# Moving the evacuation of the attention accumulators, in the first half of the keys, from VectorE to ScalarE

## What is computed

```python
def polymax(x):            # on the causal scores, 1/DIVISOR = 1e-3
    x <= 0 and x >= -100:  (-0.01 * x + 1) / 1000
    x > 0:                 (x * x + 1) / 1000

x = x + attention(layernorm(x)) @ W_proj        # 16 heads of 64, causal, polymax in place of softmax
x = x + (gelu(layernorm(x) @ U1 @ V1 + b1) @ U2 @ V2 + b2)
```

## Time and profile before

| | us |
|---|---|
| median of two runs | 2102.88 (2097.38 to 2108.37) |
| the profiled execution, its own time | 2102.51 |
| its span on the slowest core, core 3 | 2101.0 (others from 2082.8) |
| busy on that core: TensorE, VectorE, ScalarE | 1305.7, 1260.8, 760.1 |

### The profile page before, as it was taken

One profiled execution on the slowest core, in us unless ns is written; L12 is line 12 of the kernel. 1 busy time (PEld: TensorE's weight loads), 2 busy tenths in 40 slices (PEclk: granted clock), 3 DMA queues, 4 the chain that ended last, 5 costly groups with the idle time before them and its releaser, 6 DMA issues.

```text
span 2101.0 us, 22691 instructions; the slowest of 8 cores (2082.8 to 2101.0 us)
## 1 busy us (share of the span) xinstructions
PE 1305.7 (62%) x6880; PEld 459.8 (22%) x6880; DVE 1260.8 (60%) x2171; ACT 760.1 (36%) x1074; POOL 0.2 (0%) x4
## 2 busy tenths in 40 slices
PE   2423295577786776777678337666765461468886
PEld 0001042243222222212112113322221220023332
DVE  3557432234888898889889523488997233344422
ACT  1100000000656676667667300176775000033332
POOL 0000000000000000000000000000000000000000
PEclk8655597889756677778777669855666685579998
DMA  5545202200000000000000320000000443001111
GB/s 165 160 120 180 100 7 73 74 7 11 21 8 19 16 6 16 8 16 6 16 18 6 96 69 1 1 1 1 1 1 23 158 147 113 0 0 41 40 41 40
DMA packets 53334, 96.07 MB, mean 46 GB/s; under 512 B 2529, under 2 KB 24290, under 8 KB 53218
## 3 DMA queue, kind: packets, MB, share of 16 engines
q1 hardware_dynamic: 46498, 84.14, 12.6%
q10 hardware_dynamic: 6720, 10.49, 1.7%
HBM read 82.04 MB, written 12.58 MB: 45 GB/s over the span
## 4 chain that ended last, share of the span: by engine, by line
PE 46%; DVE 25%; issue 13%; DMA 11%; ACT 3%; SPq 1%; DVEq 1%; ACTq 0%
DVE poolD L765 12%; PE ps L799 8%; DMA poolD<-W_attn 6%; PE ps L731 5%; PE ps L848 4%; PE ps L1124 3%; PE ps L933 3%; PE ps L1030 3%; PE ps L632 3%; PE ps L654 3%; PE ps L612 3%; PE ps L1144 3%; DMA poolD<-W_proj 1%; DMA poolD<-x_t 1%; DVE poolC L498 1%
## 5 line engine op out<-in xcount | busy, mean ns | idle before, releaser
L752 ACT ACTIVATE poolD<-ps 128x1024 bf16<-128x1024 f32 (+3 forms) x640 | 559.9, 900 | 849.0 <-PE ps L731 737.0
L765 DVE SCALAR_TENSOR_TENSOR poolD<-poolD 128x1024 bf16<-128x1024 bf16 (+3 forms) x640 | 653.0, 1058 | 43.4 <-ACT poolD L752 20.9
L799 PE MATMUL ps<-poolD,poolA 128*64 128x512 bf16 (+3 forms) x1280 | 298.4, 454 | 223.1 <-DVE poolD L765 115.4
L731 PE MATMUL ps<-poolB,poolA 64*128 64x512 bf16 (+3 forms) x1280 | 274.1, 454 | 35.7 <-ACT poolD L757 17.9
L799 PEld LDWEIGHTS ps<-poolD,poolA 128*64 128x64 bf16 x1280 | 89.0, 117 | 403.2 <-issue 401.7
L1136 ACT ACTIVATE poolC<-ps,sb_b1s 128x512 bf16<-128x512 f32 x128 | 87.7, 687 | 113.2 <-PE ps L1124 71.6
L757 ACT ACTIVATE poolD<-ps,consts 128x256 bf16<-128x256 f32 x256 | 123.7, 483 | 0.0
L848 PE MATMUL ps<-poolC,poolD 128*128 128x512 bf16 x256 | 123.1, 481 | 0.0
L731 PEld LDWEIGHTS ps<-poolB,poolA 64*128 64x128 bf16 x1280 | 64.2, 101 | 234.3 <-issue 233.5
L933 PE MATMUL ps<-poolD,poolC 128*128 128x512 bf16 x256 | 63.4, 405 | 55.4 <-DVE poolD L905 55.4
L612 PE MATMUL ps<-poolC,poolD 128*128 128x512 bf16 x256 | 57.1, 387 | 42.0 <-DVE poolD L591 42.0
(11 more groups left out here) (101 smaller groups left out, 1142.2 us busy)
## 6 DMA issues: line engine op xcount, KB each, us to landing
poolD<-x_t SPq DMA_DIRECT2D x8, 2048.0 KB, 10.3
poolA<-x_t SPq DMA_DIRECT2D x8, 2048.0 KB, 10.6
poolD<-W_attn SPq DMA_DIRECT2D x12, 1024.0 KB, 5.0
poolD<-W_attn SPq DMA_DIRECT2D x16, 512.0 KB, 4.1
poolC<-x_own_t SPq DMA_DIRECT2D x8, 1024.0 KB, 5.1
y<-poolC SPq DMA_DIRECT2D x4, 2048.0 KB, 6.8
kf2scratch<-poolD SPq DMA_DIRECT2D x32, 128.0 KB, 1.7
poolA<-kf2scratch SPq DMA_DIRECT2D x4, 1024.0 KB, 13.8
```

Of the source, the lines that this page charges most:

```text
L731: e.matmul(o, l, r, skip_group_check=True, start=True, stop=True, tile_position=tp),
L752: e.activation(o, i, AF.Relu), inc="S")
L765: e.scalar_tensor_tensor(o, i, 0.01, i, ALU.add, ALU.mult),
L799: e.matmul(o, l, r, skip_group_check=True, start=st, stop=True, tile_position=tp),
```

## The change

In half 0 the four pieces of the accumulator are evacuated by ScalarE in place of VectorE: as an activation `Identity` with the `prefsnap` column as its bias where the addition is needed (c = 0 and 1 except j = 1), and as a multiplication by 1.0 elsewhere. VectorE keeps the copy of the K piece. Half 1 stays as it was. ScalarE waits for the last matmul of the block before the four, as VectorE does. TensorE gets waits on the S semaphore beside those on V before the accumulator bank is written again and before the output projection.

```diff
         av_free = {4: 0, 5: 0}
+        av_freeS = {4: 0, 5: 0}
...
                             b.wait("tensor", "V", av_free[avbk])
+                            b.wait("tensor", "S", av_freeS[avbk])
...
                                 b.wait("tensor", "V", av_free[idle_bk])
+                                b.wait("tensor", "S", av_freeS[idle_bk])
...
-                    b.wait("vector", "T", tfence())
+                    tf_av = tfence()
+                    b.wait("vector", "T", tf_av)
+                    if half == 0:
+                        b.wait("scalar", "T", tf_av)
...
-                        if not chunk_final:
+                        if half == 0:
+                            if chunk_final and j > 1:
+                                b.op("scalar", lambda e, o=dst, s=src,
+                                     pv=prefsnap[:, j, p:p + 1]:
+                                     e.activation(o, s, AF.Identity, bias=pv), inc="S")
+                            else:
+                                b.op("scalar", lambda e, o=dst, s=src:
+                                     e.mul(o, s, 1.0), inc="S")
+                        elif not chunk_final:
                             b.op("vector", lambda e, o=dst, s=src: e.tensor_copy(o, s),
                                  inc="V")
-                        elif c <= 1:
-                            if j == 1:
-                                b.op("vector", lambda e, o=dst, s=src: e.tensor_copy(o, s),
-                                     inc="V")
-                            else:
-                                b.op("vector", lambda e, o=dst, s=src,
-                                     pv=prefsnap[:, j, p:p + 1]:
-                                     e.tensor_scalar(o, s, pv, None, ALU.add), inc="V")
...
                     av_free[avbk] = b.cnt["V"]
+                    av_freeS[avbk] = b.cnt["S"]
...
         xo_dma(0, 1)
+        b.wait("tensor", "S", attn_done["S"])
```

## The result

The changed kernel takes 2112.76 us against 2104.78 us, medians of 43 and 42 runs. The ratio is **1.0044, with a 95% interval from 1.0027 to 1.0062**, some 9 us slower (6 to 13 by the interval), which a reader would call no change at 2%, but which is clear of noise. The forecast was 2110 us, 0.3% slower. Ratios are taken from runs in which both halves of the chip ran alike, so where a median and a ratio disagree the ratio counts. The profiled execution has a span of 2110.0 us on its slowest core, core 1, from which the rows of after are taken. Beside the lines of the changed file named ahead, L801 and L809 are the product with V, L732 the scores and L713 the cast of the K weights; L880 and L883 are ScalarE's pieces with and without a bias.

A forecast was written before the change was run, and what follows sets the result against it. Block ends were taken as bound by last product, first scores, first ReLU, then VectorE's step; ReLU delays of 2.9, 2.6 and 1.7 us sum to 7.2, and 2102.5 + 7.2 = 2109.7, forecast as 2110 us, range 2099 to 2122.

The forecast's parts named there:

- What bounds the kernel now: At block ends in half 0: chain L799, L731, ReLU L752, L765; VectorE's evacuation lies beside it, so removal gains nothing.
- How long four take: ScalarE's four pieces before the first ReLU: 0.66 us in c = 2 and 3, 0.98 in c = 1, 0.90 in c = 0.
- the estimate of 2130 us: Skill's rule for ScalarE: four pieces cost 1.6 us, some 27 us over 24 passages; given little weight.
- When they can start: ScalarE's pieces start with VectorE's K-piece copy; the first ReLU already starts 0.42, 0.54 and 0.52 us behind it by chunk.
- The sum: First-ReLU delay over 24 passages: 2.9 us in c = 0, 2.6 in c = 1, 1.7 in c = 2 and 3; 7.2 together.
- the clock of TensorE: Passages shifting against TensorE's clock changes could lengthen or shorten blocks, 3 us either way; widens the range, no separate case.
- the prediction's own last sign: Prediction is wrong if the length of the attention stage over half 0 doesn't follow the sum over the passages.
- The waits: VectorE's waits for L752 and L757 grow from 0.19 to 1.1, 1.4 and 1.6 us by chunk, some 31 us in 24 passages.
- Costed at nothing: No cost at 7 passages covered by the W_attn load (some 2 us without cover), half 0's end, TensorE's S waits, PSUM banks.
- Relief of the busiest engine: Rival at block ends: VectorE's removed pieces and short idling come back whole, some 25 us, 2077 us; chance 0.05.
- Absorbed delay: Rival: delay at a block's start disappears further in, where VectorE and ScalarE wait for TensorE anyway; about 2103 us; chance 0.15.
- Dearer evacuation: Rival: ScalarE's pieces don't overlap, each costing its duration; 2121 us, 2130 with more fixed cost; 2116 to 2130, chance 0.16.

The follow-up runs named there:

- the order in which the scores run ahead: Kernel before, scores and ReLUs three tiles ahead across block ends, copy and evacuation behind next L765: 2048.27 us, pieces on VectorE; 2026.25 us, half 0's on ScalarE.
- the earlier load: Next K weights loaded three blocks earlier: in the kernel before, 2075.72 us, ratio 0.9816; in the changed kernel, ratio 0.9850.
- the doubled pieces: Changed kernel with a second set of four ScalarE pieces, into an unused buffer, ahead of each set: ratio 1.0104 against the kernel before.
- both orders together: Kernel before with scores and ReLUs ahead across block ends and K weights loaded three blocks earlier: 1983.57 us, pieces on ScalarE; 2014.80 us on VectorE.

## Why the prediction was right

*What bounds the kernel now.* It held. VectorE's evacuation lay beside the scores and the first ReLU; taking it away altogether changed nothing, 0.9991.

*How long four take.* 0.165 and 0.245 us apiece were forecast, 0.16 and 0.25 measured. The durations, 0.28 and 0.37 as worked out, were right too but are not what the next instruction waits for. The Trainium skill's rule, "ScalarE: Activation LUTs", section "Rules for kernel authors", some 0.3 us per ACTIVATE plus 0.83 ns per element, fits the duration of a piece with a bias (0.41 against 0.37) and is too high by over half for its place in a row (0.41 against 0.25); the estimate of 2130 us worked out from it is outside the measurement.

*When they can start.* Off by 0.08 us: ScalarE starts its pieces 0.08 us ahead of VectorE's copy (1080.08 and 1080.16), not with it. That halved what was left in each passage of c = 2 and 3 and more: 0.03 us in place of 0.14, 0.4 us in place of 1.7 for twelve. In c = 0 and 1 it is 2.8 and 2.5 for 2.9 and 2.6.

*The sum.* 7.2 us were forecast. The passages measured 5.7, the whole some 9 by the time and 10.8 by the length of half 0. What the sum lacks arises inside the blocks of c = 0 and 1, 2 to 5 us by the three pairs of profiled executions. In c = 0 it goes with the clock of TensorE, which I had only in the range, at 3 us of either sign and for the passages alone; in c = 1 its cause is open. By the prediction's own last sign, that the stage's length follow the sum over the passages, the sum is not the whole account. That 2110 came within 3 us of the measurement is so partly by luck: 1.5 us too much at the passages stand against the time inside the blocks, which is not in the sum. The time itself, 6 to 13 us slower, would only just have agreed with the passages alone.

*The waits.* They should grow by some 31 us, the prediction says, but 31 is what they would come to; the growth by the same figures is 28. Measured is 26.4.

*Costed at nothing.* Right as far as the sum goes: in the passages with a load nothing was added. The aside, that each would cost as the others do once that cover went, was wrong: with the load moved away they don't pay, since the cast of the K weights then stands on VectorE between the copy and the first step and covers the delay, at 0.60 us and more. The end of half 0 and TensorE's waits show nothing: what comes behind the last copy lasts 913.1 us before and 912.6 after.

*The rivals.* Relief of the busiest engine failed in this order of the work and came true in the order in which the scores run ahead: 22 us with 24 passages and 31 us with 31 (though not in c = 1). In small it came true at the 7 passages where the earlier load had made VectorE the bound. Absorbed delay is excluded by the doubled pieces in c = 1 to 3, and by the steps of the changed kernel, which keep the delay to the end of the block. Dearer evacuation is excluded by the starts of the pieces.

## What to carry to other kernels

An engine's busy share does not tell what an instruction on it is worth; look at what ends the wait right behind the instruction. If that is another engine, moving the work there makes it late. When an engine is to be relieved, first take away what it waits for: the same move cost 9 us before that and gained 22 to 31 after it. The pieces behind the first ReLUs on ScalarE in the old order were not tried, but there was nothing to gain by it: even leaving them out altogether gave 0.9991. Instructions in a row cost the next one the distance of their starts, which for these short ones was 0.16 of 0.28 us and 0.25 of 0.37. And a sum over the places that an edit touches is to be compared with the length of the stage as well: here half of the added time lay elsewhere.

## What was not expected of the hardware

The granted clock of TensorE in c = 0 changes from kernel to kernel, and not in one direction: 0.69 with the kernel before, 0.63 with 0.46 us more in each passage, 0.70 with 1.4 us more (means over the eight cores of one execution; the doubled pieces for the last). Executions of kernels whose passages in c = 0 are those of before gave 0.69, 0.69 and 0.67, and 0.65 with the earlier load; with the pieces on ScalarE it was 0.63 and 0.65, and 0.65 with the earlier load. So part of this is the spread between executions, and that the length of the stops decides it is not shown. What the engine did before each change of its level was not followed up, so why it goes down and up again stays open.

What is shown is the price. In c = 0 of every kernel in the old order the length of the chunk goes with the clock over the eight cores (the correlation is -0.60 in the least clear one and -0.88 to -0.99 in the others), for instance 98.0 us at 0.68 and 102.8 at 0.58 in the changed one.

Where the stops at the passages are gone, the granted clock in c = 3 is higher: 0.86 and 0.90 with the scores ahead and the pieces on VectorE and on ScalarE, 0.83 and 0.95 with both orders together, against 0.77 in the kernel before (means over the eight cores). Why is open too.
